# A graph network's first layer adds its rows into three copies of the sums in place of four

## What is computed

```python
h = relu(layernorm(x))
# first layer: for each edge, a weighted feature row of its dst is added to its src
x = x + segment_sum(edge_weight[:, None] * (h @ W)[dst], src, 12500)
h = relu(layernorm(x))
# second layer: attention with 8 heads over the edges of each dst, then a projection
x = x + attention(h, src, dst, Wq, bq, Wk, bk, Wv, bv) @ Wo.T + bo
```

## Time and profile before

| | |
|---|---|
| median of the runs | 7130.53 us |
| span of the profiled execution | 7184.9 us |
| busy in it: GpSimd | 4666.6 us (65%) |
| TensorE matmul | 4609.9 us (64%) |
| VectorE | 4538.0 us (63%) |
| ScalarE | 3961.0 us (55%) |
| DMA moved | 1130.07 MB, mean 157 GB/s |

### The profile page before, as it was taken

One profiled execution on the slowest core, in us unless ns is written; L12 is line 12 of the kernel. 1 busy time (PEld: TensorE's weight loads), 2 busy tenths in 40 slices (PEclk: granted clock), 3 DMA queues, 4 the chain that ended last, 5 costly groups with the idle time before them and its releaser, 6 DMA issues. The chain is left out here.

```text
span 7184.9 us, 117508 instructions
## 1 busy us (share of the span) xinstructions
PE 4609.9 (64%) x19717; PEld 3407.0 (47%) x19717; DVE 4538.0 (63%) x12295; ACT 3961.0 (55%) x14482; POOL 4666.6 (65%) x3716
## 2 busy tenths in 40 slices
PE   1456666666666666657885666676666766766767
PEld 1344444444444445544553444454444544544545
DVE  4665555555555666655546767777666767776766
ACT  0655555555555555533334666666666666666661
POOL 1488888888888888885554555666565655665630
PEclk6677777777777777778997887888877888888779
DMA  8777777777777777778754665666665666666646
GB/s 310 179 105 105 105 105 106 106 105 108 105 108 108 107 108 109 109 94 295 259 190 138 172 173 167 185 179 182 181 182 172 183 183 188 183 186 188 193 134 194
DMA packets 644181, 1130.07 MB, mean 157 GB/s; under 512 B 74529, under 2 KB 466795, under 8 KB 643445
## 3 DMA queue, kind: packets, MB, share of 16 engines
q0 software_dynamic: 367600, 678.97, 48.4%
q1 hardware_dynamic: 223985, 273.78, 11.8%
q10 hardware_dynamic: 51860, 169.74, 7.2%
HBM read 929.80 MB, written 451.51 MB: 192 GB/s over the span
## 5 line engine op out<-in xcount | busy, mean ns | idle before, releaser
L701 POOL DMA_INDIRECT sums<-mtw,posIw x1563 | 2490.8, 1594 | 599.4 <-issue 416.2
L1249 POOL DMA_INDIRECT kv<-kvt,sI x1760 | 1802.6, 1024 | 1247.1 <-issue 1107.1
L1610 ACT ACTIVATE room<-kv,pp 128x33 f32<-128x33 f32 x8800 | 1921.3, 308 | 47.8 <-issue 43.4
L1525 PE MATMUL ps<-room,Of 128*128 128x264 f32 x3520 | 1193.8, 484 | 619.6 <-DVE acc L1713 455.5
L734 PE MATMUL ps<-h,wf 128*128 x3320 | 1225.0, 524 | 307.1 <-DVE mtw L825 238.5
L718 PE MATMUL ps<-Mw,Oh 128*128 128x128 f32 x3320 | 671.9, 368 | 916.5 <-DVE Oh L852 908.7
L1525 PEld LDWEIGHTS ps<-room,Of 128*128 128x128 f32 x3520 | 760.4, 233 | 911.8 <-issue 585.3
L825 DVE SCALAR_TENSOR_TENSOR mtw<-mtw,cont,ps 128x256 f32 x1660 | 794.6, 479 | 621.2 <-SPq L690 448.1
L718 PEld LDWEIGHTS ps<-Mw,Oh 128*128 128x128 f32 x3320 | 631.5, 274 | 1033.8 <-DVE Oh L852 993.9
L734 PEld LDWEIGHTS ps<-h,wf 128*128 128x128 f32 x3320 | 818.5, 263 | 589.2 <-issue 450.0
L799 ACT COPY wf<-ps 128x512 f32<-128x512 f32 x415 | 242.8, 585 | 1237.8 <-PE ps L718 933.3
(11 more groups left out here) (223 smaller groups left out, 4741.1 us busy)
## 6 DMA issues: line engine op xcount, KB each, us to landing
qb<-qt SPq DMA_DIRECT2D x880, 192.0 KB
accd<-acc SPq DMA_DIRECT2D x880, 132.0 KB
ints<-srows ACTq DMA_DIRECT2D x205, 512.0 KB
OT<-drows SPq DMA_DIRECT2D x110, 512.0 KB
sums<-zero ACTq DMA_DIRECT2D x72, 704.0 KB
part<-sums SPq DMA_DIRECT2D x56, 896.0 KB
kv<-kvt,sI POOLq DMA_INDIRECT x1760
kvt<-kvo SPq DMA_DIRECT2D x98, 260.0 KB
```

The costliest lines, as they stand in the source:

```text
L701: e.indirect_dma_start(sums[t % NS], bass.IndirectOffsetOnAxis(ap=posI[:, t % NP:t % NP + 1], axis=0), mt[:, t % NM, :], None, compute_op= ...
L1249: e.indirect_dma_start(kv[:, s % NK, :], None, kvt, bass.IndirectOffsetOnAxis(ap=sI[:, s:s + 1], axis=0)).then_inc(kvs.sem(s), 16)
L1525: m = e.matmul(psum[6 + j % 2][:, 0:NH * 33], lhsT=Of[:, w % 2, k % W2, :], rhs=pv[:, k % NV, :], start=(k % 2 == 0), stop=(k % 2 == 1))
L1610: e.activation(pv[:, s % NV, h * 33:h * 33 + 33], kv[:, s % NK, D + h * 33:D + h * 33 + 33], ACT.Copy, scale=pp[:, w % 2, h, s % W2:s % W2 ...
```

## The change

NS goes from 4 to 3. Three copies of the sums are zeroed, added to and loaded. The wait at L700 is now for tile t - 3. ScalarE's loops issue the zeros of copies 0 and 1 in the preparation as before, and of copy 2 alone in the first layer's block. In the middle `rest` is gone, and `half` adds copy 2 to copy 1. BACK, NM, the order of the loads and everything in the second layer stay.

```diff
-NS = 4
+NS = 3
...
-                for k in range(NS // 2):
+                for k in range(NS - 1):
                     zeros(e, k)
...
-                for k in range(NS // 2, NS):
+                for k in range(NS - 1, NS):
                     zeros(e, k)
                 norm(0)
...
                 def half(g):
                     e.wait_ge(pload.sem(g * NS), pload.value(g * NS + NS - 1))
-                    e.tensor_tensor(part[:, g % 3, 2, :, :], part[:, g % 3, 2, :, :], part[:, g % 3, 3, :, :],
-                                    ALU.add).then_inc(S("b_half"), 1)
-
-                def rest(g):
-                    e.wait_ge(S("b_half"), 2 * g + 1)
                     e.tensor_tensor(part[:, g % 3, 1, :, :], part[:, g % 3, 1, :, :], part[:, g % 3, 2, :, :],
                                     ALU.add).then_inc(S("b_half"), 1)
 
                 half(0)
-                rest(0)
...
-                    if t % G == 3 and g + 1 < NG7:
-                        rest(g + 1)
...
                 def whole(g):
                     e.wait_ge(pload.sem(g * NS), pload.value(g * NS + NS - 1))
-                    e.wait_ge(S("b_half"), 2 * g + 2)
+                    e.wait_ge(S("b_half"), g + 1)
```

## The result

The changed kernel takes 7179.69 us (median of 4 runs, 7173.35 to 7190.44), the kernel before 7129.97 us beside it (4 runs). The medians differ by 49.7 us, where 41.5 us were forecast. The ratio of the runs is 1.0067, with an interval of 1.0051 to 1.0083, which is 48 us.

What follows compares the result with a forecast made beforehand. GpSimd's scatters were taken to bound the first layer, ScalarE's queue its head, TensorE the middle. +108 - 35.5 - 9 - 22 = +41.5 us on 7130.5 gave 7172 us; forecast 7150 to 7200, range 7095 to 7235 us.

Steps and rivals of the forecast that it cites:

- Part 1: First layer's scatters: waiting for tile t - 3 lets late landings delay GpSimd; +108 us, bounds +13 to +175 us.
- the limit: First layer: with three copies, a tile needing more than 4.9 us to land delays GpSimd; with four, 6.8 us.
- The 0.7 us from wait to start: First layer: time between the end of the landing wait and the scatter's start, if GpSimd has run dry.
- the scatters' slowing: First layer: scatters take 52 us over their undisturbed time; a GpSimd standing still can't be slowed, so 9 us come off.
- my pairing: First layer: starts paired with landings; 188 tiles too late for three copies, 0.62 us in the mean, 117 us together.
- Part 2: Head of the first layer: ScalarE issues 18 DMAs of zeros in place of 36; -35.5 us, -25 to -40 us.
- the bound that I named, the loads: Head of the first layer: if loads of x and edge rows arrived last, some 10 us of the gain would stay out.
- Parts 3 and 4: The middle: `rest` and one load go; -9 us at its head, -22 us in its steady part.
- The head of the middle: Before the first product: `rest` (3.96 us) and one load (3.1 us) go, the second group gains; -9 us, -4 to -14.
- the 2 us for the second group: Head of the middle: the second group, where TensorE waits 6.50 us, gets its data two loads earlier; 2 us gained.
- The steady part: The middle's later groups: one load fewer ahead of the stores shortens VectorE's waits; -22 us, 0 to -34 us.
- A: Rival, first layer: late landings don't bite as the hand-over is mostly hidden; sum -36 us, 7094 us; chance 0.12.

Runs made afterwards that it cites:

- The moved zeros: The kernel before, four copies, but ScalarE issues zeros of three copies in the preparation, of one in the first layer's block; 7155.89 against 7168.57 us.
- the experiment: The kernel before, all four copies loaded, but without GpSimd's second addition (`rest`) in the middle; 0.9999 of the kernel before, 6352.4 us.

## Why the prediction was right

**What bounds the first layer.** Right: what was added to GpSimd's time came out at the end in full, and VectorE, with 448 us of waiting in hand, only waited longer.

**Part 1.** The mechanism, the limit and the number of cases were right: 188 late landings forecast, 196 waits measured. The 0.7 us from wait to start rested on one tile and proved exact: 0.70 us here, and 0.23 us as soon as the order of the waits was changed. The size was a little low, +108 against +129 and +110 us in two executions. Of its two terms, the scatters' slowing gave back 14 us (I had 9), and the waits cost 145 and 119 us beyond the usual 0.30 us (I had 117). Between these two executions the late tiles explain it: 90% had landed after 5.57 and 5.45 us, and each tenth of a us at the limit is worth 20 us over 196 tiles. They don't explain the miss against the first, since in the trace of before 90% had landed after 5.57 us too. Added up over all tiles, what landings took beyond 4.9 us was 168 us before, 177 and 149 us after, and the waits cost about 0.8 of it both times; the same share of before's 168 us would have been some 136 us, where my pairing gave 117. It laid the landings against the starts of the old kernel, whose slowed scatters already stand further apart than 1.86 us; that this is why it came out low is not shown.

**Part 2.** The size was right: 35.5 forecast, 35.8 by ScalarE's queue; the other 5 us of the stage's 40.9 I hadn't forecast, and no run here explains them. The reason was right in part. ScalarE issues its zeros while they fill the DMA engines, at 398 to 420 GB/s from 140 to 190 us before, and I hadn't read that: the bytes and the queue go together. The moved zeros show the bound that I named, the loads, at work as soon as the bytes stay.

**Parts 3 and 4.** The head of the middle gained 6.5 us (9 forecast). `rest` gave its 4.0 us and the load 2.5 us: `half` starts 23.9 us after the last scatter before and 21.4 us after. I had 3.1 us for the load from the 12.23 us of the earlier trace rows, which are the issues of the second group, not of the first; the 2 us for the second group didn't come on top. The steady part, from the first to the last `whole`, went from 405.3 to 373.7 us: -31.6, where I had -22 from an upper bound of -34. This term was mis-sized: I took two thirds since several of the 11 waits are shorter than the 3.1 us that a load takes. The 3.1 us were right in the steady part (4.95 to 1.77 us for a group's issues), and VectorE's waits shrank by 25 us, about as I had it. But ScalarE's wait for the stores of the queries, in the same queue, shrank too, from 30.8 to 7.7 us, and I hadn't counted it. That `rest` was worth nothing there was right, and the experiment bears it out. The Trainium skill's rule that the two engines exclude each other ("SBUF — State Buffer", section "SBUF: two separate sides") is not against it. The trace of before agrees with the rule: L436 runs beside `half` in nine groups and takes 3.70 us in eight of them, as after. But it never runs beside `rest`, which holds up only a small L1175 in two groups, by some 0.3 us each.

**The rivals.** A, that the landings don't bite because the hand-over is hidden, was the opposite of what happened; yet the swapped waits come close to that kernel, at -42 us where A had -36, with 0.23 us of the hand-over left. The Trainium skill's fit for a DMA ("DMA: Bandwidth & Descriptors", section "Anatomy of one DMA — SWDGE (gpsimd) path"), 2.0 us and the bytes at 436 GB/s, gives 2.3 us for a tile. With the 1.56 us of the instruction that is an estimate of 3.9 us, and the median of 3.87 us agrees with it. The fit has no term for a tile that shares the DMA engines with a load, and those decided here, at 5.5 to 5.8 us. All three terms came out larger than forecast, one that adds to the time (by 21 us) and two that take from it (by 5 and 7 us), and so the sum was off by only 8 us. That it was so near is luck: the misses cancelled, and 5 us of them are the head's that nothing explains.

## What to carry to other kernels

How many buffers a chain of accumulating DMAs needs is decided not by its usual landing but by its late ones: compare buffers times the issue period, less the hand-over, with the landing beside the largest other transfer. Where a wait may be the last one to end before an engine's instruction, write it so that the instruction itself carries it; here that was two lines in another order, and worth some 90 us of 7180. And compare stage by stage before believing two spans.

## What was not expected of the hardware

A wait that the scatter carries hands over in 0.23 us, one that stands ahead of it as an instruction in 0.70 us.

The second layer, with the same instructions, took 3128 to 3185 us beside the result and on the first chip, and 2346 to 2367 us on the other, while the first layer and the middle took the same time everywhere. Windows of the kernel without `rest`, on the other chip:

```profile
405.00:3222.00 2817.00, 1739.05 (x6264) 1358.96 (x6264) 1655.56 (x6863) 1499.86 (x3886) 2365.04 (x1483) 0.74 0.72 106
3741.00:6104.00 2363.00, 1910.08 (x10676) 1372.54 (x10675) 2212.33 (x3630) 2025.32 (x9403) 1825.95 (x1869) 0.94 0.81 241
```

Against the third row of the windows after, TensorE's granted clock is 0.94 in place of 0.81 and the DMA engines are busy for 0.81 of the time in place of 0.62; VectorE (2212 against 2233 us) and ScalarE (2025 against 2036 us) work nearly as long, and their idle time is what is gone. What the engines wait for in the slower case was not settled. Whole times are compared above only between kernels that ran beside each other.
